# A graph-attention kernel on one core: the product with Wv of each group moved one turn later on TensorE

## The chip, the cores and the metric

The kernel runs on one core of one Trainium2 chip. The metric is the device time of one execution in microseconds (us), and the median of several runs is compared. The program is written by hand, engine by engine, with semaphores between the engines; no scheduler reorders it. The engines are named as the profile names them: PE (TensorE), ACT (ScalarE), DVE (VectorE), POOL (GpSimd, which here only issues gathers and scatters) and SP (which issues the plain DMAs).

## The reference

`x` has 100000 rows of 128 numbers, and 25000 edges run between those rows. Cut to what matters:

```
feat   = concat([h[dst], h[src], rel_pos, distance])          # per edge
z      = silu(silu(feat @ W1 + b1) @ W2 + b2)
scores = (z @ W3 + b3)[:, 0]
alpha  = softmax of the scores over the edges of one receiving row
msg    = h[src] @ Wv * (alpha * node_weight[src])[:, None]
out    = segment_sum(msg, dst)                                 # add up by receiving row
x      = layernorm(x + h + out)                                # h is x
```

So most rows are only normalised (the dense part), and the rows that receive an edge get a sum of weighted messages first.

## The kernel before

The edges are padded to 49 groups of 512 (four tiles of 128). In a first stage (turns `i`, loops over `B0`) the sender rows are gathered, multiplied with the part of W1 that belongs to them and written to DRAM, while DVE sorts the edges by receiver. In the second stage, which the change touches, the sorted edges go through a pipeline of `LAST_STEP` = 66 turns `s`. Every engine has its own loop over the same `s`, and within an engine the order of the code is the order of the work. In turn `s` PE does, for different groups, in this order:

- `krow` (L606) of group s-9: the receivers' numbers are spread over the one bank 4, from which DVE's `weights` makes the matrix `m_q`. It waits for `m_ready` of the group before, because bank 4 is the only one;
- the scores (L616) of group s-3; they wait for `x2_ready`, and in the first turn of a new batch of four groups for `s_taken`, that is until DVE's `take_scores` has read bank 3;
- the product with W2 (L623) of group s-2 and the two parts of the product with W1 (L629, L631) of group s-1;
- in one turn of four, the transpose of alpha (L639);
- z (L645) of group s-10, the sum of the weighted sender rows, into bank 5;
- the transposes of the rows of group s+1 (L596, in `turn_rows`), which ACT copies to `hkT`;
- y (L654) of group s-10, the product of z with Wv, into bank 6. It waits for ACT's copy `zs` of bank 5 (L520) of this same turn and for `y_done`, DVE's read of bank 6.

ACT does in a turn: the copy `hkT` (L500), four normalised rows of the dense part (L477), the second silu (L505, waits for the W2 product and for the scores), four more, the first silu (L510), in one turn of four an exponential (L515), the copy `zs` (L520, waits for z), five more of L477, and four rows of results (L529).

DVE does in a turn, in this order: `take_scores` (L943, one turn of four), `dense_norm` (L920), `rows` of group s-11 (L982 and L987, waits for `y_ready`), the first half of the softmax (L950 to L953, one turn of four), `dense_stats` (eight of L905, in nearly all turns up to turn 34), `weights` of group s-9 (four of L973, waits for `krow_ready`; its last one gives `m_ready`), the second half of the softmax (L959 to L964), and what is left of the running chains (short instructions of L876 to L890, some of which also lie between the others). So `rows` in turn s uses the y that PE made at the end of turn s-1.

POOL issues four gathers `r` of a later group (L415, region) once the W2 product of the third group before is done (`R_AHEAD`), then four gathers `hk` (L415, hk), and from group 39 on four scatters of results (L419) in their place. A scatter of group k waits for z of group k+25 or for the last one (`SC_AHEAD`), so the scatters that are left when the last z is done stand at the very end of the kernel. A block of the dense part comes in eight turns of nine (`DSTEP`), from the start of the second stage to turn 34.

Of the kernel before, what the change touches and what calls it, by code (L numbers as in the profile page):

```python
# [11 lines left out]
P = 128  # L12
# [3 lines left out]
TPG = 4  # L16
GE = TPG * P
G = -(-E // GE)
# [17 lines left out]
Y_LAG, Z_LAG, M_LAG = 11, 10, 9  # L36
# [81 lines left out]
def group_tiles(b):  # L118
    return min(BT, T - b * BT)


def gnn_kernel(nc, x, xw, snd_nat, rcv_nat, id_nat, signs, iota, ef_flat, w1, b1, w2, b2, w3, b3, wv, eye, out):
# [9 lines left out]
    with ExitStack() as ctx:  # L132
        def sb(name, shape, dt=F32):
            return ctx.enter_context(nc.sbuf_tensor(name, shape, dt))
# [8 lines left out]
        wvh = sb("wvh", [P, H])  # L143
# [20 lines left out]
        zs = sb("zs", [P, GE])  # L164
# [73 lines left out]
        bank = [ctx.enter_context(nc.psum_tensor(f"bank{n}", [P, GE], F32)) for n in range(8)]  # L238
# [23 lines left out]
        def wait(eng, s, n):  # L262
            if n > 0:
                eng.wait_ge(S[s], n)

        def wait_ring(eng, ring, i, per):

            if i >= 0:
                eng.wait_ge(ring[i % len(ring)], (i // len(ring) + 1) * per)
# [8 lines left out]
        def batch_of(g):  # L278
            return g // BATCH

        def batch_end(b):
            return min(b * BATCH + BATCH, G) - 1
# [260 lines left out]
        def _(pe):  # L543
# [24 lines left out]
            for i in range(B0):  # L568
                j = i - 2
                if 0 <= j < G:  # L570
# [3 lines left out]
                    for q in range(TPG):  # L574
                        to = bank[2 + j % 4][:, q * P:(q + 1) * P]
                        pe.matmul(to, hsT[:, j % 2, q * P:(q + 1) * P], w1b[:], start=True, stop=False)  # L576
                        ins = pe.matmul(to, ef[0:36, j % EF_RING, q * P:(q + 1) * P], w36[:], start=False, stop=True)  # L577
                    ins.then_inc(S["A_ready"], 1)
                if i < G:
                    wait_ring(pe, hs_in, i, 16 * TPG)  # L580
                    wait(pe, "hsT_ready", i - 1)
                    for q in range(TPG):
                        ins = pe.transpose(bank[i % 2][:, q * P:(q + 1) * P], rec[:, i % HS_RING, q, H:2 * H], ident[:])  # L583
# [8 lines left out]
            def turn_rows(g):  # L592
                wait_ring(pe, hk_in, g, 16 * TPG)
                wait(pe, "hkT_ready", g)
                for q in range(TPG):
                    ins = pe.transpose(bank[0][:, q * P:(q + 1) * P], hk[:, g, q, :], ident[:])  # L596
                ins.then_inc(S["hkT_done"], 1)

            turn_rows(0)
            for s in range(LAST_STEP):  # L600
                g = s - M_LAG
                if 0 <= g < G:
                    wait(pe, "m_ready", g)
                    for q in range(TPG):
                        t = g * TPG + q
                        ins = pe.matmul(bank[4][:, q * P:(q + 1) * P], kcol16[:, t:t + 1].to_broadcast((P, P)), ident16[:],  # L606
                                        start=True, stop=True)
                    ins.then_inc(S["krow_ready"], 1)
                g = s - 3
                if 0 <= g < G:  # L610
                    b, last = batch_of(g), g == batch_end(batch_of(g))
                    wait(pe, "x2_ready", g + 1)
                    wait(pe, "s_taken", b)
                    for q in range(TPG):
                        n = (g % BATCH) * TPG + q
                        ins = pe.matmul(bank[3][0:BT, 0:P], wz[:, BT - 1 - n:2 * BT - 1 - n], x2[:, q * P:(q + 1) * P],  # L616
                                        start=(n == 0), stop=(last and q == TPG - 1), skip_group_check=True)
                    ins.then_inc(S["score_done"], 1)
                g = s - 2
                if 0 <= g < G:  # L620
                    wait(pe, "x1_ready", g + 1)
                    wait(pe, "x2_ready", g)
                    pe.matmul(bank[2][:], w2s[:], x1[:], start=True, stop=True).then_inc(S["mm2_done"], 1)  # L623
                g = s - 1
                if 0 <= g < G:
                    wait(pe, "hkT_ready", g + 1)
                    wait_ring(pe, r_in, g, 16 * TPG)
                    wait(pe, "x1_ready", g)
                    pe.matmul(bank[1][:], w1a[:], hkT[:, g % 2, :], start=True, stop=False, skip_group_check=True)  # L629
                    for q in range(TPG):  # L630
                        ins = pe.matmul(bank[1][:, q * P:(q + 1) * P], rr[:, g % R_RING, q, 0:H], ident[:], is_transpose=True,  # L631
                                        start=False, stop=(q == TPG - 1), skip_group_check=True)
                    ins.then_inc(S["mm1_done"], 1)
                for b in range(NBATCH):
                    if batch_end(b) + 5 == s:
                        n = group_tiles(b)
                        wait(pe, "alpha_ready", b + 1)
                        wait(pe, "acol_ready", b)
                        pe.transpose(bank[7][:, 0:n], soft[0:n, 5, :], ident[0:n, 0:n]).then_inc(S["alphaT_done"], 1)  # L639
                g = s - Z_LAG  # L640
                if 0 <= g < G:
                    wait(pe, "m_ready", g + 1)
                    wait(pe, "zs_ready", g)
                    for q in range(TPG):
                        ins = pe.matmul(bank[5][:, q * P:(q + 1) * P], rr[:, g % R_RING, q, H:2 * H], m_q[:, g % 2, q, :],  # L645
                                        start=True, stop=True)
                    ins.then_inc(S["z_ready"], 1)
                if s + 1 < G:
                    turn_rows(s + 1)
                if 0 <= g < G:  # L650
                    wait(pe, "zs_ready", g + 1)
                    wait(pe, "y_done", g)
                    for q in range(TPG):
                        ins = pe.matmul(bank[6][:, q * P:(q + 1) * P], zs[:, q * P:(q + 1) * P], wvh[:], start=True, stop=True)  # L654
                    ins.then_inc(S["y_ready"], 1)

            pe.wait_ge(S["fix_in"], 16 * 11)
            for k in range(2):
                pe.transpose(bank[k][:, 0:P], yrow[:, 2 * k, :], ident[:])
                ins = pe.transpose(bank[k][:, P:T], yrow[0:T - P, 2 * k + 1, :], ident[0:T - P, 0:T - P])  # L660
# [460 lines left out]
```

## Time and profile before

| | |
|---|---|
| three runs | 1179.71, 1186.98, 1191.53 us; median 1186.98 us |
| profiled execution | 1186.11 us, of which the span that the trace covers is 1177.9 us |
| busy | PE 635.3, DVE 586.4, ACT 523.2, POOL 752.8 us |
| TensorE clock granted, mean | 0.81 |

No engine is busy for more than two thirds of the span, so waits between engines set the time. The page's 40 slices of 29.4 us each show the stages: up to slice 13 the first stage, slices 14 to 26 the second stage with dense work, from 27 on the second stage without it, and in the last five slices only POOL's scatters.

### The profile page before, as it was taken

Reading aid. Unit: us, or ns where it says so; the run is one execution under the profiler, and the core shown is the slowest. Engines: PE = TensorE matmul, PEld = TensorE weight load, DVE = VectorE, ACT = ScalarE, POOL = GpSimd, SP = SyncE. Lnnn points to the kernel's source line nnn. Section 1 sums busy time; section 2 is a strip of 40 time slices with the busy share of each in tenths; the row PEclk is TensorE's granted clock in tenths of the full one; section 3 lists DMA queues with packets and bytes.
Section 4 is the critical chain, followed back from the end, with each engine's and each line's share of the span. In section 5 each row is a group of like instructions: output and inputs, shape, how many; then the busy total and the mean of one; then the engine's idle time right before and its main releaser. Section 6 shows DMA issues by size and latency. Waiting matters only on the chain.

```text
span 1177.9 us, 11360 instructions
## 1 busy us (share of the span) xinstructions
PE 635.3 (54%) x2783; PEld 436.6 (37%) x2783; DVE 586.4 (50%) x2276; ACT 523.2 (44%) x1168; POOL 752.8 (64%) x790
## 2 busy tenths in 40 slices
PE   2388778869703445666755766665555636610000
PEld 1256555546401222444434544444344425610000
DVE  4587665564431544597657766853323135532000
ACT  0255354355522556567667858765334324340000
POOL 7566666666677565656646656664656665577775
PEclk9999999999999976787877777787778777655555
DMA  6388877879974486575747566742212211121111
GB/s 207 101 257 289 256 261 245 275 263 253 292 240 147 162 287 235 165 249 188 243 159 242 200 214 213 245 143 81 72 55 68 68 54 40 44 71 52 53 51 38
DMA packets 77913, 199.67 MB, mean 170 GB/s; under 512 B 18999, under 2 KB 49398, under 8 KB 65304
## 3 DMA queue, kind: packets, MB, share of 16 engines
q1 hardware_dynamic: 49560, 134.47, 32.0%
q0 software_dynamic: 28288, 64.48, 20.4%
q8 instruction: 23, 0.38, 0.1%
q14 instruction: 42, 0.34, 0.1%
HBM read 106.74 MB, written 92.26 MB: 169 GB/s over the span
## 4 chain that ended last, share of the span: by engine, by line
PE 22%; ACT 21%; issue 18%; another core or an unknown queue 18%; POOL 10%; DVE 7%; SPq 2%; DMA 2%; ACTq 0%; POOLq 0%; DVEq 0%
ACT xin L477 12%; POOL out_rows L419 10%; PE bank L576 8%; PE bank L583 3%; ACT hk L529 3%; PE bank L577 3%; PE bank L654 2%; DVE dst L905 2%; PE bank L616 2%; PE bank L623 1%; DMA xin<-in_x 1%; ACT x L510 1%; ACT zs L520 1%; ACT hkT L500 1%
## 5 line engine op out<-in xcount | busy, mean ns | idle before, releaser
L415 POOL DMA_INDIRECT region<-rec_d,id_t x196 | 186.5, 952 | 172.4 <-PE bank L623 53.0
L477 ACT ACTIVATE xin<-xin,drs 128x128 f32<-128x128 f32 x637 | 257.9, 484 | 52.9 <-issue 32.4
L415 POOL DMA_INDIRECT hk<-in_xw,snd_t x196 | 189.9, 969 | 102.6 <-issue 54.9
L419 POOL DMA_INDIRECT out_rows<-hk,sidx_t x196 | 188.7, 963 | 76.4 <-issue 57.8
L415 POOL DMA_INDIRECT hk<-in_x,kg_t x196 | 185.5, 946 | 66.1 <-issue 58.8
L654 PE MATMUL bank<-wvh,zs 128*128 128x128 f32 x392 | 86.5, 389 | 215.6 <-ACT zs L520 151.3
L576 PE MATMUL bank<-w1b,region 128*128 128x128 f32 x392 | 151.3, 489 | 66.3 <-issue 43.7
L905 DVE BATCH_NORM_STATS2 dst<-xin 128x6 f32<-128x256 f32 x392 | 137.6, 416 | 67.1 <-DMA xin<-in_x 50.1
L654 PEld LDWEIGHTS bank<-wvh,zs 128*128 128x128 f32 x392 | 73.4, 280 | 227.2 <-ACT zs L520 159.3
L576 PEld LDWEIGHTS bank<-w1b,region 128*128 128x128 f32 x392 | 99.1, 313 | 91.8 <-issue 56.0
L982 DVE TENSOR_TENSOR hk<-bank,hk 128x512 f32<-128x512 f32 x49 | 33.8, 689 | 185.0 <-PE bank L654 79.4
L616 PE MATMUL bank<-x,wz 128*16 128x128 f32 x392 | 79.3, 372 | 26.7 <-ACT x L505 15.9
L505 ACT ACTIVATE x<-bank,bcol 128x512 f32<-128x512 f32 x49 | 33.6, 686 | 129.4 <-remote 105.9
L487 ACT ACTIVATE region<-bank 128x512 f32<-128x512 f32 x49 | 28.9, 590 | 138.9 <-PE bank L583 61.3
L623 PE MATMUL bank<-x,w2s 128*128 128x512 f32 x98 | 72.0, 824 | 19.9 <-ACT x L510 19.3
L529 ACT ACTIVATE hk<-hk,ers 128x128 f32<-128x128 f32 x196 | 79.8, 483 | 4.6 <-issue 3.2
L973 DVE TENSOR_SCALAR m_q<-bank,kcol,acol 128x128 f32<-128x128 f32 x196 | 73.4, 403 | 2.4 <-remote 2.2
L629 PE MATMUL bank<-hkT,w1a 128*128 128x512 f32 x98 | 55.2, 647 | 20.3 <-DMA region<-rec_d,id_t 19.4
L616 PEld LDWEIGHTS bank<-x,wz 128*16 128x16 f32 x392 | 45.6, 127 | 50.2 <-issue 18.8
L583 PE MATMUL bank<-ident,hk 128*128 128x128 f32 x196 | 54.3, 432 | 16.0 <-DMA w<-hk 16.0
L645 PE MATMUL bank<-m_q,region 128*128 128x128 f32 x392 | 59.3, 297 | 1.7 <-issue 1.6
L510 ACT ACTIVATE x<-bank,bcol 128x512 f32<-128x512 f32 x49 | 33.2, 677 | 57.3 <-remote 34.7
(179 smaller groups left out, 913.0 us busy)
## 6 DMA issues: line engine op xcount, KB each, us to landing
xin<-in_x SPq DMA_DIRECT2D x49, 1024.0 KB
out_rows<-xin SPq DMA_DIRECT2D x49, 1024.0 KB
rec_d<-hk SPq DMA_DIRECT2D x49, 514.0 KB
hk<-in_xw,snd_t POOLq DMA_INDIRECT x196
hk<-in_x,kg_t POOLq DMA_INDIRECT x196
region<-rec_d,id_t POOLq DMA_INDIRECT x196
out_rows<-hk,sidx_t POOLq DMA_INDIRECT x196
ef_d<-hk SPq DMA_DIRECT2D x9, 196.0 KB
```

Of the source, the lines that this page charges most:

```text
L415: pool.indirect_dma_start(out=to, out_offset=None, in_=frm, in_offset=bass.IndirectOffsetOnAxis(ap=index, axis=0)).then_inc(done, 16)
L419: pool.indirect_dma_start(out=out, out_offset=bass.IndirectOffsetOnAxis(ap=index, axis=0), in_=frm, in_offset=None).then_inc(done, 16)
L477: ins = nc.scalar.activation(xin[:, j % X_RING, n, :], xin[:, j % X_RING, n, :], ACT.Identity, bias=drs[:, j % 2, 1, n:n + 1], scale=drs[: ...
L529: ins = nc.scalar.activation(hk[:, g, q, :], hk[:, g, q, :], ACT.Identity, scale=ers[:, b % 2, 0, n:n + 1], bias=ers[:, b % 2, 1, n:n + 1])
L576: pe.matmul(to, hsT[:, j % 2, q * P:(q + 1) * P], w1b[:], start=True, stop=False)
L583: ins = pe.transpose(bank[i % 2][:, q * P:(q + 1) * P], rec[:, i % HS_RING, q, H:2 * H], ident[:])
L616: ins = pe.matmul(bank[3][0:BT, 0:P], wz[:, BT - 1 - n:2 * BT - 1 - n], x2[:, q * P:(q + 1) * P], start=(n == 0), stop=(last and q == TPG ...
L623: pe.matmul(bank[2][:], w2s[:], x1[:], start=True, stop=True).then_inc(S["mm2_done"], 1)
L645: ins = pe.matmul(bank[5][:, q * P:(q + 1) * P], rr[:, g % R_RING, q, H:2 * H], m_q[:, g % 2, q, :], start=True, stop=True)
L654: ins = pe.matmul(bank[6][:, q * P:(q + 1) * P], zs[:, q * P:(q + 1) * P], wvh[:], start=True, stop=True)
L905: ins = vec.bn_stats(dst[:, n:n + 2, :].rearrange("p j w -> p (j w)"), xin[:, j % X_RING, n:n + 2, :].rearrange("p j h -> p h j"))
L973: ins = vec.tensor_scalar(m_q[:, g % 2, q, :], bank[4][:, q * P:(q + 1) * P], kcol[:, t:t + 1], acol[:, b % 2, n:n + 1], ALU.is_equal, ALU ...
```

## The change

Y is issued one turn later: in turn s for group s-11 in place of s-10, and at another place in the turn, after the product with W1 and ahead of the transpose of alpha and of z. Its two waits stay (the copy `zs` of its group, and DVE's read of the group before from bank 6). The banks stay as they are: one for z, one for y, one for `krow`.

```diff
@@ -631,6 +631,13 @@
                         ins = pe.matmul(bank[1][:, q * P:(q + 1) * P], rr[:, g % R_RING, q, 0:H], ident[:], is_transpose=True,
                                         start=False, stop=(q == TPG - 1), skip_group_check=True)
                     ins.then_inc(S["mm1_done"], 1)
+                g = s - Z_LAG - 1
+                if 0 <= g < G:
+                    wait(pe, "zs_ready", g + 1)
+                    wait(pe, "y_done", g)
+                    for q in range(TPG):
+                        ins = pe.matmul(bank[6][:, q * P:(q + 1) * P], zs[:, q * P:(q + 1) * P], wvh[:], start=True, stop=True)
+                    ins.then_inc(S["y_ready"], 1)
                 for b in range(NBATCH):
                     if batch_end(b) + 5 == s:
                         n = group_tiles(b)
@@ -647,12 +654,6 @@
                     ins.then_inc(S["z_ready"], 1)
                 if s + 1 < G:
                     turn_rows(s + 1)
-                if 0 <= g < G:
-                    wait(pe, "zs_ready", g + 1)
-                    wait(pe, "y_done", g)
-                    for q in range(TPG):
-                        ins = pe.matmul(bank[6][:, q * P:(q + 1) * P], zs[:, q * P:(q + 1) * P], wvh[:], start=True, stop=True)
-                    ins.then_inc(S["y_ready"], 1)
 
             pe.wait_ge(S["fix_in"], 16 * 11)
             for k in range(2):
```

The order of one turn of the second stage on PE, before, from `krow` to the next `krow` (the bracket holds the semaphores that the first instruction of a group waits for):

```order
L606 MATMUL bank<-ident,kcol 128x128 [waits m_ready]
L606 MATMUL bank<-ident,kcol 128x128 x3
L616 MATMUL bank<-x,wz 16x128 [waits s_taken,x2_ready]
L616 MATMUL bank<-x,wz 16x128 x3
L623 MATMUL bank<-x,w2s 128x512 [waits x2_ready,x1_ready]
L629 MATMUL bank<-hkT,w1a 128x512 [waits x1_ready,r_in4,hkT_ready]
L631 MATMUL bank<-ident,region 128x128 x4
L645 MATMUL bank<-m_q,region 128x128 [waits zs_ready,m_ready]
L645 MATMUL bank<-m_q,region 128x128 x3
L596 MATMUL bank<-ident,hk 128x128 [waits hkT_ready,hk_in2]
L596 MATMUL bank<-ident,hk 128x128 x3
L654 MATMUL bank<-wvh,zs 128x128 [waits y_done,zs_ready]
```

And the same stretch with the change, where y is L639 and z is L652:

```order
L606 MATMUL bank<-ident,kcol 128x128 [waits m_ready]
L606 MATMUL bank<-ident,kcol 128x128 x3
L616 MATMUL bank<-x,wz 16x128 [waits s_taken,x2_ready]
L616 MATMUL bank<-x,wz 16x128 x3
L623 MATMUL bank<-x,w2s 128x512 [waits x2_ready,x1_ready]
L629 MATMUL bank<-hkT,w1a 128x512 [waits x1_ready,r_in9,hkT_ready]
L631 MATMUL bank<-ident,region 128x128 x4
L639 MATMUL bank<-wvh,zs 128x128 [waits y_done,zs_ready]
L639 MATMUL bank<-wvh,zs 128x128 x3
L652 MATMUL bank<-m_q,region 128x128 [waits zs_ready,m_ready]
L652 MATMUL bank<-m_q,region 128x128 x3
L596 MATMUL bank<-ident,hk 128x128 [waits hkT_ready,hk_in7]
```

The four matmuls of y have gone from behind the transposes L596 to between the W1 product and z: before they stood directly ahead of `krow`, now `krow`, the scores and the products with W2 and W1 stand ahead of them in their turn.

In the turn that transposes alpha, with the change (L646 is that transpose; before, it stood directly behind L631):

```order
L629 MATMUL bank<-hkT,w1a 128x512 [waits x1_ready,r_in7,hkT_ready]
L631 MATMUL bank<-ident,region 128x128 x4
L639 MATMUL bank<-wvh,zs 128x128 [waits y_done,zs_ready]
L639 MATMUL bank<-wvh,zs 128x128 x3
L646 MATMUL bank<-ident,soft 128x16 [waits acol_ready,alpha_ready]
L652 MATMUL bank<-m_q,region 128x128 [waits zs_ready,m_ready]
```

Here y stands ahead of the one instruction in the turn that waits for the end of the softmax on DVE. On the other engines nothing moves.

## Rows read from the trace of the kernel before

**Rows 1.** Windows: stretch, length, busy of PE, PEld, DVE, ACT, POOL, clock, DMA, GB/s
```profile
491.00:784.00 293.00, 185.38 (x946) 131.57 (x946) 214.80 (x834) 207.87 (x472) 178.41 (x188) 0.77 0.62 210
784.00:983.00 199.00, 112.60 (x592) 79.14 (x591) 62.83 (x204) 75.53 (x146) 119.97 (x125) 0.75 0.24 70
```
**Rows 2.** Waits of the whole span: who waited for whom, total, times, longest
```profile
PE bank L654 <- ACT zs L520: 151.3, 34, 18.9
ACT x L505 <- remote: 105.9, 25, 9.8
```
**Rows 3.** Timeline of PE, one dense turn: start, us, engine, line, operation
```profile
671.79 2.07 PE L654 MATMUL bank<-wvh,zs 128*128 128x128 f32 x8 [3.39 <-issue]
673.65 0.63 PE L606 MATMUL bank<-ident,kcol 128*128 128x128 bf16 x4
...
675.54 1.13 PE L623 MATMUL bank<-x,w2s 128*128 128x512 f32 x2
...
677.79 1.06 PE L645 MATMUL bank<-m_q,region 128*128 128x128 f32 x8
...
684.00 2.08 PE L654 MATMUL bank<-wvh,zs 128*128 128x128 f32 x8 [4.72 <-ACT zs L520]
```
**Rows 4.** Timeline of PE, the slowest and the fastest krow-to-z seen
```profile
698.17 0.63 PE L606 MATMUL bank<-ident,kcol 128*128 128x128 bf16 x4
...
703.89 1.16 PE L645 MATMUL bank<-m_q,region 128*128 128x128 f32 x8
...
887.11 1.16 PE L654 MATMUL bank<-wvh,zs 128*128 128x128 f32 x8 [0.25 <-ACT zs L520]
888.10 0.39 PE L606 MATMUL bank<-ident,kcol 128*128 128x128 bf16 x4
...
891.65 1.06 PE L645 MATMUL bank<-m_q,region 128*128 128x128 f32 x8
```
**Rows 5.** Timeline of ACT over the same dense turn
```profile
671.16 0.58 ACT L520 ACTIVATE zs<-bank 128x512 f32<-128x512 f32 x1
...
680.68 0.69 ACT L505 ACTIVATE x<-bank,bcol 128x512 f32<-128x512 f32 x1 [3.46 <-remote]
```
**Rows 6.** Timeline of DVE: a plain turn, one without dense work, one with softmax
```profile
662.47 0.69 DVE L982 TENSOR_TENSOR hk<-bank,hk 128x512 f32<-128x512 f32 x1 [1.13 <-issue]
...
667.90 0.42 DVE L973 TENSOR_SCALAR m_q<-bank,kcol,acol 128x128 f32<-128x128 f32 x1
...
670.12 0.17 DVE L890 SCALAR_TENSOR_TENSOR drs<-dst,drs 128x16 f32<-128x16 f32 x1
...
673.90 0.69 DVE L982 TENSOR_TENSOR hk<-bank,hk 128x512 f32<-128x512 f32 x1 [2.70 <-PE bank L654]
...
675.30 1.35 DVE L973 TENSOR_SCALAR m_q<-bank,kcol,acol 128x128 f32<-128x128 f32 x4
680.62 0.34 DVE L943 TENSOR_SCALAR soft<-bank,bcol 16x128 f32<-16x128 f32 x1 [3.96 <-remote]
686.12 0.69 DVE L982 TENSOR_TENSOR hk<-bank,hk 128x512 f32<-128x512 f32 x1 [5.16 <-PE bank L654]
...
694.54 0.41 DVE L973 TENSOR_SCALAR m_q<-bank,kcol,acol 128x128 f32<-128x128 f32 x1
```
**Rows 7.** Timeline of DVE: L982 of turns 35 and 50
```profile
783.78 0.69 DVE L982 TENSOR_TENSOR hk<-bank,hk 128x512 f32<-128x512 f32 x1 [4.04 <-PE bank L654]
...
983.48 0.69 DVE L982 TENSOR_TENSOR hk<-bank,hk 128x512 f32<-128x512 f32 x1 [4.79 <-PE bank L654]
```
**Rows 8.** Timeline of POOL: the first r gathers two turns apart, a scatter
```profile
669.18 0.94 POOL L415 DMA_INDIRECT region<-rec_d,id_t  x1 [2.55 <-PE bank L645]
...
693.62 0.94 POOL L415 DMA_INDIRECT region<-rec_d,id_t  x1 [2.45 <-PE bank L645]
...
1031.93 0.96 POOL L419 DMA_INDIRECT out_rows<-hk,sidx_t  x1 [2.02 <-remote]
```
**Rows 9.** Source L982: all rows instructions, first and last start
```profile
L982 DVE TENSOR_TENSOR hk<-bank,hk x49: 668/691/693, 491.3 to 1038.0; 128x512 f32<-128x512 f32 x49
```

## The prediction

> **What bounds the kernel now.** I read the page first (no engine is busy for more than two thirds of the span), then the windows by stage, the waits, and the timeline of single turns on PE, ACT, DVE and POOL. The change touches only the second stage. From turn 11 on it has three parts. The dense part runs from the first rows instruction (L982) at 491.3 [rows 9] to that of turn 35 at 783.78 [rows 7]: 24 turns in 292.5 us, 12.2 us a turn. The part without dense work runs from there to turn 50 at 983.48: 15 turns in 199.7 us, 13.3 a turn. The last turns run to turn 59 at 1038.0 [rows 9]: 9 turns in 54.5 us, 6.1 a turn. In the first two parts PE's mean granted clock is 0.77 and 0.75 of full [rows 1], so PE changes between its two levels of 2.4 and 1.2 GHz all the time.
>
> The wait that the change removes is the longest of the table: PE's y waits for ACT's copy zs for 151.3 us in 34 waits [rows 2]. What does it hold up? In a dense turn ACT ends zs at 671.74; y starts at 671.79 [rows 3, 5], `krow` only at 673.65, behind y, and behind that come the scores and the W2 product, for which ACT's L505 then waits 3.46 us [rows 5]. Such waits of L505 are 105.9 us in 25 [rows 2]. Today's loop is thus: zs, y, krow, scores, W2 (PE), then L505, four norms, L510, zs (ACT).
>
> **What the change takes away.** With y of the group before, PE can do krow, the scores and W2 without ACT's zs of the same turn. ACT's own work of a dense turn is what is left of 12.2 us without the wait of 3.5: 8.7 us. If ACT set the pace, that would be the turn.
>
> **What it puts in its place.** DVE's loop is not moved. In its turn s, `rows` (L982) waits for y, and `weights` (L973) of the same turn comes behind it; `krow` of PE's turn s+1 waits for `m_ready` of these weights, since bank 4 is one. Before, the y that rows of turn s needs stood at the end of PE's turn s-1, ahead of krow. Now it stands in turn s, behind krow, scores, W2 and W1. So these follow each other with nothing beside them: PE krow to y (call it P), DVE rows to the last weights (D), PE krow of the next turn. Z and the transposes L596 lie beside D.
>
> D comes from the timeline of DVE [rows 6]: a plain dense turn 662.47 to 668.32, 5.8 us; a turn without dense work 673.90 to 676.65, 2.75 us; a turn with the softmax 686.12 to 694.95, 8.8 us. All of this is work or its own short chains, and L982 has no price of its own that changes (49 of about 0.69 us).
>
> P is krow, scores, W2 and W1, then y. Krow to z, which is that stretch without y, takes 3.55 us at the full clock (888.10 to 891.65) and 5.72 at its slowest (698.17 to 703.89) [rows 4]; in the turn of [rows 3] 4.14 (673.65 to 677.79). Y takes 1.0 at the full clock (887.11 to the krow behind it at 888.10) and 1.86 at half (671.79 to 673.65). So P lies between 4.6 and 7.6 us; I take 6.5, nearer to the slow end, because the mean clock is 0.77 and because ends reach others late (below). Its lower end stays the lower end of the range.
>
> Sum for the 24 dense turns. Of these, turns 17 and 26 have no dense work (every ninth), and turns 11, 15, 19, 23, 27 and 31 have the softmax:
> - 16 plain turns at 6.5 + 5.8 = 12.3: 197 us.
> - 6 with the softmax at 6.5 + 8.8 = 15.3, and 1.8 more: in these turns the scores wait for `take_scores`, which stands behind the rest of DVE's chain. The weights end at 668.32 and that chain at 670.29 [rows 6], L943 takes 0.34, so it is done 2.3 us after `m_ready`, of which krow's start covers 0.5. Together 17.1: 103 us.
> - 2 turns at 6.5 + 2.75 = 9.25, but POOL's eight gathers of a turn take 1.25 each, 10.0 us: 20 us.
>
> That is 320 us against 292.5: 27 us slower. The cover of the softmax turns was that rows never waited on the same turn's PE work; it is gone. ACT (8.7 a turn) and POOL (10.0) become the ones that wait.
>
> In the 15 turns without dense work the loop is 6.5 + 2.75 = 9.3 us (about 11 with the softmax), under the 13.3 they take. What fills those 13.3 is POOL's eight issues of 1.26 (10.1 us) and long waits on PE that I can't put down to one instruction. I cost the edit at nothing there; the bounds are -10 (a fifth of the wait was zs) and +20 (y adds its 1.0 to 1.9 on P in 13 of them, uncovered).
>
> In the last 9 turns PE only has krow, y and z. Today z, zs (0.58), y and krow follow each other, 6.1 us a turn. With the change krow, y, rows and weights do: 0.4 + 1.2 + 2.75, some 4.4 to 5.5 by the clock. But POOL issues a scatter group per turn, 4 of 1.26 = 5.0 us. I take half a microsecond a turn, 4 us less. This counts in full: at 1031.93 a scatter waits 2.02 us for PE [rows 8], and from there POOL issues without a gap to the end, so whatever moves z of the last group moves the end.
>
> The sum: +27 - 4 = +23 us. Against the profiled execution of 1186.1 us (span 1177.9 and 8.2 around it) that is 1209; that execution lies 0.9 under the median of the runs, 1186.98. Against the median it is 1210.
>
> On the clock, the trace shows 0.77 as the mean while PE is busy for 63% of the dense part [rows 1], and y takes 1.86 us in one turn and 1.0 in another [rows 3, 4]. The Trainium skill (TensorE: Matmul & The Clock Gate, Part 1) says that an array left idle falls to half its clock and that activity gives the full one back. It speaks against this change, because the loop makes PE stand still once a turn until DVE has the weights; by that rule P would sit at its slow end, and that case has its place among the rivals.
>
> **The rivals.**
> - *A, faster: ACT sets the pace after all.* P at its fast end, 4.6. Then plain turns are 4.6 + 5.8 = 10.4 (166 us for 16), softmax turns 4.6 + 8.8 + 1.8 = 15.2 (91), two of 10: 277, 15 less than now. With 8 less in the last turns it is 1164. For it: the longest wait goes. Against: the clock.
> - *B, no change: POOL keeps its beat.* The first r gathers of a turn start at 669.18 and, two turns later, at 693.62, 12.2 us a turn, though between them lie a turn with a D of 2.75 and the start of one with 8.8 [rows 6]; each time POOL waits about 2.5 us for PE [rows 8]. If that beat has a cause that I don't see, plain turns stay at 12.2 and the softmax turns' excess is made up in the others: 1187, from 1176 to 1198.
> - *C, the forecast:* the PE-DVE loop, 1199 to 1228.
> - *D, much slower: y's end comes late.* The W2 product's record ends at 676.67 and L505, which waits for it and for the scores ahead of it, starts at 680.68, 4.0 us later [rows 3, 5]. Y, with zs ahead of it, is read at once today. In the changed order y stands in the same run as W2, with W1's 1.1 to 1.3 us and its own 1.0 to 1.9 in between, so that 1.5 us of the lateness is left, in each of 24 turns: 36 more than the forecast, 1246. It decides as soon as y's end lags by more than the 0.5 us that P at 6.5 has over the sum of its rows (4.14 + 1.86).
> - *E: PE at half its clock in all of P.* P 7.6 at the slowest row: 1.1 more in 24 turns, 26: 1236.
>
> That the edit doesn't do what it says is no case: y of a group always finds its zs a turn old, and its two waits stay.
>
> **Chances.** A 0.20, B 0.24, C 0.33, D 0.16, E 0.07. A measurement of this kernel tells about 1% (12 us) from no change. Faster by over 1% is A: 0.20. Within 1% is B and a sliver of C: 0.26. Slower by over 1% is the rest: 0.54. The likeliest case gives 1210; its own range is 1199 to 1228. The range that should hold 8 in 10 leaves out half of A below and the top of D above: 1168 to 1248.
>
> **What the profile after would show.** The wait of y for zs near nothing, and in its place PE's krow waiting for DVE's L973; DVE's L982 waiting for y nearly every turn of the dense part, with 12.3 us between two of them in plain turns and 17 in turns with the softmax; L505's waits shorter or put down to krow's lateness; POOL waiting for the W2 product for longer. If rows come 10.4 apart in plain turns, A is right; if all turns stay 12.2 apart, B; if they are 13.5 or more apart with y's record ended 1.5 us before L982 starts, D. I would be wrong in the mechanism if krow doesn't wait for DVE.

## The result and the profile after

The changed kernel takes 1217.6 us (median of 4 runs, 1212.1 to 1222.0); the kernel before took 1187.8 beside it (4 runs, 1179.7 to 1191.5). The ratio is 1.029, with a 95% interval from 1.024 to 1.034: 30 us slower, where the likeliest case said 23. The profiled execution is the slowest of the four, 1222.0 us with a span of 1214.5, so the two traces differ by 36.6 us, more than the medians. TensorE's mean clock is 0.79 (0.81 before).

Where the 36.6 us are is read from DVE's `rows`, the same instruction as in [rows 7, 9] (from here on the lines of DVE are one higher, y is L639 and z L652). Its first and last start:

```profile
L983 DVE TENSOR_TENSOR hk<-bank,hk x49: 669/692/693, 488.0 to 1074.1; 128x512 f32<-128x512 f32 x49
```

Turn 35 now starts at 824.8 and turn 50 at 1019.8. The window of the dense part, with the columns of [rows 1]; the clock in it is 0.74, where it was 0.77:

```profile
488.00:825.00 337.00, 203.80 (x967) 129.30 (x967) 214.40 (x834) 218.95 (x488) 184.19 (x195) 0.74 0.56 188
```

The dense part took 336.8 us for 24 turns, 44.3 more than before (forecast 27). The part without dense work took 194.9, 4.8 less (forecast 0); the last turns 54.3, 0.3 less (forecast 4). The start of the stage came 3.3 earlier and the end of the kernel 0.5 later; together that is 36.6. So the whole loss lies in the dense turns. Of the 44 us, 8 come from y's end being seen late in two of them (told with rival D below).

The waits answer to [rows 2]; "remote" is a releaser that the trace doesn't name. Columns: who waited for whom, total us, times, longest:

```profile
PE bank L606 <- DVE m_q L974: 116.8, 26, 14.3
DVE hk L983 <- PE bank L639: 116.7, 29, 7.3
DVE hk L983 <- remote: 116.2, 11, 15.8
...
PE bank L606 <- issue: 100.9, 19, 12.0
...
ACT x L505 <- remote: 36.6, 9, 6.4
...
ACT x L505 <- PE bank L623: 29.5, 19, 3.2
```

The 151 us of y waiting for `zs` are gone from the head of the table (15.0 are left), and L505 waits less: it had 105.9 us under this releaser, now 36.6, and 29.5 of short ones (0.9 us in a plain turn) for the W2 product. In their place PE's `krow` waits for DVE's weights (the row with "issue" too: in the turns below it starts 0.06 us behind them), and DVE's rows wait for y. One plain turn and the start of a softmax turn on PE, against [rows 3]:

```profile
745.87 0.61 PE L606 MATMUL bank<-ident,kcol 128*128 128x128 bf16 x4 [4.66 <-issue]
746.40 1.89 PE L616 MATMUL bank<-x,wz 128*16 128x128 f32 x8
748.22 2.08 PE L623 MATMUL bank<-x,w2s 128*128 128x512 f32 x2
750.09 1.91 PE L629 MATMUL bank<-hkT,w1a 128*128 128x512 f32 x2
751.80 0.70 PE L631 MATMUL bank<-ident,region 128*128 128x128 f32 x4
752.33 1.06 PE L639 MATMUL bank<-wvh,zs 128*128 128x128 f32 x8
...
759.16 0.61 PE L606 MATMUL bank<-ident,kcol 128*128 128x128 bf16 x4 [4.44 <-issue]
761.48 1.86 PE L616 MATMUL bank<-x,wz 128*16 128x128 f32 x8 [1.72 <-issue]
```

And DVE over the same time, against [rows 6]:

```profile
745.40 0.41 DVE L974 TENSOR_SCALAR m_q<-bank,kcol,acol 128x128 f32<-128x128 f32 x1
753.42 0.69 DVE L983 TENSOR_TENSOR hk<-bank,hk 128x512 f32<-128x512 f32 x1 [4.76 <-PE bank L639]
758.70 0.40 DVE L974 TENSOR_SCALAR m_q<-bank,kcol,acol 128x128 f32<-128x128 f32 x1
761.00 0.33 DVE L944 TENSOR_SCALAR soft<-bank,bcol 16x128 f32<-16x128 f32 x1
767.79 0.69 DVE L983 TENSOR_TENSOR hk<-bank,hk 128x512 f32<-128x512 f32 x1 [5.68 <-PE bank L639]
```

Read the two side by side. The last weights end at 745.81, `krow` starts at 745.87. Y's record ends at 753.39, rows start at 753.42. The weights end at 759.10, `krow` starts at 759.16. Each waits for the other, with nothing of the loop beside it (z and the transposes L596 lie beside D, as foreseen): P (krow to the end of y) is 7.5 us, D (rows to the last weights) 5.7. The scores start at 761.48, behind `take_scores` (L944), 1.7 us late.

### The profile page after: what moved, and what is told of

Read it like the earlier page. It is cut to its first block, busy times and chain, and to the rows that moved or that the text cites. A ratio compares the mean times of both kernels' runs of the same rounds, so it can differ in the third digit from the quotient of the medians.

```text
span 1214.5 us, 11360 instructions
## 1 busy us (share of the span) xinstructions
PE 640.9 (53%) x2783; PEld 422.9 (35%) x2783; DVE 586.0 (48%) x2276; ACT 526.9 (43%) x1168; POOL 752.6 (62%) x790
## 4 chain that ended last, share of the span: by engine, by line
PE 22%; DVE 20%; issue 16%; another core or an unknown queue 12%; POOL 8%; ACT 4%; DMA 1%; DVEq 0%; POOLq 0%; SPq 0%; ACTq 0%
POOL out_rows L419 8%; PE bank L623 5%; PE bank L616 4%; DVE dst L906 4%; PE bank L629 3%; DVE m_q L974 3%; PE bank L639 3%; ACT xin L477 2%; DVE hk L983 2%; PE bank L606 2%; PE bank L631 1%; DVE est L988 1%; PE bank L652 1%; PE bank L576 1%
## 5 line engine op out<-in xcount | busy, mean ns | idle before, releaser
L983 DVE TENSOR_TENSOR hk<-bank,hk 128x512 f32<-128x512 f32 x49 | 33.9, 691 | 257.9 <-PE bank L639 116.7
L606 PE MATMUL bank<-ident,kcol 128*128 128x128 bf16 x196 | 26.4, 279 | 219.9 <-DVE m_q L974 116.8
L606 PEld LDWEIGHTS bank<-ident,kcol 128*128 128x128 bf16 x196 | 15.3, 120 | 230.8 <-DVE m_q L974 122.9
L623 PE MATMUL bank<-x,w2s 128*128 128x512 f32 x98 | 88.4, 999 | 12.8 <-issue 12.5
L629 PE MATMUL bank<-hkT,w1a 128*128 128x512 f32 x98 | 72.0, 827 | 32.4 <-DMA region<-rec_d,id_t 26.8
L974 DVE TENSOR_SCALAR m_q<-bank,kcol,acol 128x128 f32<-128x128 f32 x196 | 73.3, 402 | 0.3
L520 ACT ACTIVATE zs<-bank 128x512 f32<-128x512 f32 x49 | 28.9, 590 | 99.7 <-remote 72.4
L639 PE MATMUL bank<-wvh,zs 128*128 128x128 f32 x392 | 58.3, 296 | 15.7 <-ACT zs L520 15.0
L652 PE MATMUL bank<-m_q,region 128*128 128x128 f32 x392 | 59.7, 296 | 6.5 <-issue 6.5
L505 ACT ACTIVATE x<-bank,bcol 128x512 f32<-128x512 f32 x49 | 33.6, 685 | 67.4 <-remote 36.6
```

Source lines behind the costliest of these rows:

```text
L974: ins = vec.tensor_scalar(m_q[:, g % 2, q, :], bank[4][:, q * P:(q + 1) * P], kcol[:, t:t + 1], acol[:, b % 2, n:n + 1], ALU.is_equal, ALU ...
```

## The experiments

The kernels were timed in four series, each beside the kernel before. That one took 1180 us in the series of `stats_behind`, `before_stats_behind`, `lag12` and `y_scores`, 1184 in that of `weights_first`, `lag12_wfirst`, `y_end` and `warm`, 997 in that of `early_take`, `wfirst_take_alpha` and `lag12_wfirst_take_alpha`, and 1181 beside `wfirst_take_alpha_2`; the 997 are taken up below. The changed kernel itself was timed only beside the 1188, with a ratio of 1.029. So a difference from it is given by the ratios, as a share of 1188 us; the medians alone can differ from that by some 8 us. "Dense part" is the time from the first rows instruction to that of turn 35.

**Dense statistics behind the weights, on the changed kernel.**
```diff
-                dense_stats(u)
                 if 0 <= s - M_LAG < G:
                     weights(s - M_LAG)
+                dense_stats(u)
```


> The changed kernel, with DVE's eight dense_stats instructions put behind weights in its turn; nothing is left out. Theory (PE-DVE loop: krow to y on PE, then rows to weights on DVE): D falls from 5.8 to about 2.8 us in plain turns, so a plain turn falls from 13.4 us to about 10.5, where POOL's eight gathers (10.1) take over; the turns with the softmax keep about 16, since take_scores now comes behind more work. The 24 dense turns fall from 337 us to about 285, the time to about 1165 (1155 to 1185). Rival (the clock of PE or ACT's later copies set the 13.4 us): the order inside DVE doesn't matter, 1210 to 1225.

Measured: 1190.8 us, ratio 1.012 (1.005 to 1.020). The dense part fell from 336.8 to 308.5 us. Of the forecast 52 us, 27 came by the medians and 20 by the ratios: the plain turns did shrink, the softmax turns did not. DVE, with rows (L983) and weights (L974):

```profile
510.90 0.69 DVE L983 TENSOR_TENSOR hk<-bank,hk 128x512 f32<-128x512 f32 x1 [10.65 <-remote]
...
520.19 0.69 DVE L983 TENSOR_TENSOR hk<-bank,hk 128x512 f32<-128x512 f32 x1 [0.27 <-PE bank L639]
521.79 1.37 DVE L974 TENSOR_SCALAR m_q<-bank,kcol,acol 128x128 f32<-128x128 f32 x4
530.44 0.69 DVE L983 TENSOR_TENSOR hk<-bank,hk 128x512 f32<-128x512 f32 x1 [0.83 <-remote]
531.84 1.35 DVE L974 TENSOR_SCALAR m_q<-bank,kcol,acol 128x128 f32<-128x128 f32 x4
538.49 0.33 DVE L944 TENSOR_SCALAR soft<-bank,bcol 16x128 f32<-16x128 f32 x1
546.17 0.69 DVE L983 TENSOR_TENSOR hk<-bank,hk 128x512 f32<-128x512 f32 x1 [6.59 <-PE bank L639]
```

D is now 3.0 us, and two plain turns are 10.3 apart. In the first of them DVE's own work fills 9.4 us (520.19 to 529.61), so DVE is near its own bound there. The first turn of the part is 23.2 us long: y's record ended at 498.87, and DVE stood for 10.65 us before it started rows at 510.90. Such late ends add up to 16.3 us in the dense part, against 9.2 in the changed kernel. And the statistics now stand between the weights and `take_scores` of the next turn, which starts 5.3 us behind the end of the weights (1.9 in the changed kernel); the scores wait for it, and the next turn is 15.7.

**The same edit on the kernel before**, as a control.

> The kernel before, with the same move of dense_stats behind weights; nothing is left out. A control. Theory: before the change DVE's rows-to-weights path was not in the loop that sets the turn (zs, y, krow, scores, W2, L505), so the time stays at 1175 to 1195. If DVE's order were worth as much here as in the changed kernel (50 us), the loop would not be what the change brought in.

Measured: 1176.8 us, ratio 0.998 (0.994 to 1.003). No change, as the theory has it: before the change, D isn't in the loop that sets the turn.

**Rows one turn later as well**, which opens the loop at y (y stands behind the transpose of alpha here, so that no engine waits in a circle).
```diff
-Y_LAG, Z_LAG, M_LAG = 11, 10, 9
+Y_LAG, Z_LAG, M_LAG = 12, 10, 9
```


> The changed kernel with rows (and all that follows it: its chain, results, stores) one turn later (Y_LAG 12), so that rows in turn s uses the y of turn s-1; y also stands behind the transpose of alpha, without which the last batches would wait for each other. PE still doesn't wait for zs of its own turn. Theory: the PE-DVE loop is open, and krow waits only for weights that wait for no y of the same turn. A plain turn goes to 10 to 11 us (POOL's 10.1, ACT's 8.7), the time to 1150 to 1180. Rival 1 (POOL keeps a beat of 12.2 whatever PE does): 1180 to 1192, as before the change. Rival 2 (y's place in the run of PE is what costs): 1210 to 1225.

Measured: 1166.0 us, ratio 0.990 (0.983 to 0.997): by the ratios 47 us less than the changed kernel, and a little under the kernel before. Rows no longer wait for the same turn's PE work: most plain turns are 8.5 to 9.5 us.

**The weights ahead of rows**, which opens the loop at `krow` (with them the multiplication that makes `acol`).
```diff
+                if 0 <= s - M_LAG < G:
+                    weights(s - M_LAG)
                 if 0 <= s - Y_LAG < G:
                     rows(s - Y_LAG)
...
-                if 0 <= s - M_LAG < G:
-                    weights(s - M_LAG)
```


> The changed kernel with DVE's weights (and the copy of alpha's column that they need) ahead of rows in its turn. PE is as in the change: y behind W1. Theory: krow of the next turn waits for weights, and these no longer wait for y, so the loop is open; a plain turn goes to POOL's bound or to the 12.2 us that the kernel before keeps, the time to 1160 to 1190. Rival (y's place on PE is what costs): 1210 to 1225.

Measured: 1168.1 us, ratio 0.987 (0.980 to 0.993). DVE of this kernel:

```profile
618.00 0.68 DVE L983 TENSOR_TENSOR hk<-bank,hk 128x512 f32<-128x512 f32 x1
625.89 1.36 DVE L974 TENSOR_SCALAR m_q<-bank,kcol,acol 128x128 f32<-128x128 f32 x4
627.21 0.69 DVE L983 TENSOR_TENSOR hk<-bank,hk 128x512 f32<-128x512 f32 x1
```

A plain turn is 9.2 us, against 13.1 to 13.6 in the changed kernel, with the same work on every engine. In that turn ACT is busy for 9.19 of 9.20 us, so ACT sets it. By the ratios the gain on the changed kernel is 50 us. What stays long are the turns at the softmax (most of them 13.1 to 16, the first 22.2).

**Both openings together.**

> Both openings together: rows one turn later and weights ahead of rows. Theory: once the loop is open, opening it twice gives little; the next bound is POOL's gathers and its wait for PE, as in lag12: 1155 to 1175, within 1% of lag12. Rival (DVE's order still holds krow up in the turns with the softmax): 15 to 25 us less than lag12, 1140 to 1150.

Measured: 1165.1 us, ratio 0.985 (0.979 to 0.991), within the intervals of either alone. One loop was there; opened at either end it is gone, and a second opening finds nothing.

**Y directly behind the scores**, so that W2 and W1 leave P.
```diff
                     ins.then_inc(S["score_done"], 1)
+                g = s - Z_LAG - 1
+                if 0 <= g < G:
+                    wait(pe, "zs_ready", g + 1)
+                    wait(pe, "y_done", g)
+                    ...
                 g = s - 2
```


> The changed kernel with y directly behind the scores, ahead of the W2 and W1 products. Theory: P, the stretch from krow to y on PE, falls by W2 and W1, 3.5 to 4 us of 7.5; a plain turn goes from 13.4 to about 10.2 (POOL's bound), the time to 1155 to 1180. Rival (it is the wait of rows for anything in the same turn, through ACT's zs, that costs): y now comes earlier and meets zs sooner, so PE waits for zs again as before the change, 1187 or more.

Measured: 1193.8 us, ratio 1.013 (1.005 to 1.020), slower than the expected 1155 to 1180. With P shorter by W2 and W1, plain turns should have come near 10; most came at 12.2. PE, DVE and POOL show why (here y is L624, W2 L630):

```profile
728.68 2.08 PE L624 MATMUL bank<-wvh,zs 128*128 128x128 f32 x8
730.55 1.20 PE L630 MATMUL bank<-x,w2s 128*128 128x512 f32 x2
```
```profile
733.16 0.69 DVE L983 TENSOR_TENSOR hk<-bank,hk 128x512 f32<-128x512 f32 x1 [3.43 <-remote]
```
```profile
721.70 0.95 POOL L415 DMA_INDIRECT region<-rec_d,id_t  x1 [2.57 <-PE bank L630]
...
730.47 0.94 POOL L415 DMA_INDIRECT hk<-in_x,kg_t  x1 [0.30 <-issue]
733.93 0.94 POOL L415 DMA_INDIRECT region<-rec_d,id_t  x1 [2.52 <-PE bank L630]
```

Y's record ends at 730.76, rows start at 733.16, 2.4 us later. W2 ends at 731.75, POOL sees it at 733.9. POOL's eight gathers (721.70 to 731.41) and a pause of 2.5 make 12.2: the beat of rival B, in a kernel whose PE-DVE loop is shorter. The PE-DVE loop with its late end comes to about as much there (P 3.9, 2.4 until rows start, D 5.6: 12.0), so which of the two holds the turn isn't separated.

**Y at the end of the turn** (up to turn 49), behind z and the transposes, so that P grows by both.

> The changed kernel with y (still of group s-11) at the end of PE's turn, behind z and the transposes, up to turn 49; from turn 50 on it stands where the change put it. Theory (PE-DVE loop): the stretch from krow to y grows by z and the transposes, about 2 us in each of 24 dense turns; plain turns 15.4 instead of 13.4 us, the time 1245 to 1265. Rival (the change costs because y stands ahead of z and so delays zs and the results): putting it behind z gives the time back, 1185 to 1215.

Measured: 1264.3 us, ratio 1.070 (1.063 to 1.078). The dense part took 367 us. The size came as expected, not its split. P did not grow by 2 us: it was 7.8 to 8.1 in plain turns, most of which were 13.6 to 13.9 apart. So z and the transposes added 1.3 us ahead of y, but the first part of W1 (L629) took 1.02 at the full clock, where it took 1.91 in the changed kernel. The two turns at the softmax were 16 and 18, and one turn was 20, in which y was seen 9.6 us late.

**PE kept busy through its standstill:** ten matmuls of constants (64 by 384, bf16) into an unused part of bank 3 behind the transposes in each turn. They add work that the result doesn't use (where `warm16` is set up isn't shown).
```diff
                 if s + 1 < G:
                     turn_rows(s + 1)
+                if 7 <= s < G + 9:
+                    for _ in range(10):
+                        pe.matmul(bank[3][64:P, P:4 * P], ident16[:, 0:64], warm16[:], ...)
```


> The changed kernel with ten additional bf16 matmuls (64x384, into a quarter of bank 3 that nothing reads) behind the transposes of every turn, in the time in which PE stands waiting for DVE's weights. Nothing is left out. In the trace of the change krow, scores, W2 and W1 run at the half clock (krow to y 7.5 us). If the clock falls because PE stands still there, the added work keeps it up: P falls towards 4.9 us, plain turns from 13.4 to 11 or 12.2, the time to 1160 to 1195, at a higher mean clock. If the clock is not set by that standstill, nothing changes or the added work costs: 1215 to 1235.

Measured: 1209.9 us, ratio 1.025 (1.016 to 1.033), against 1.029 (1.024 to 1.034) without them: a gain in time isn't shown, and the expected 1160 to 1195 was missed. The turns can be read all the same. The mean clock from 488 to 780 us rose from 0.74 to 0.82. PE, two turns of this kernel (y is L640, the added ones L660):

```profile
732.00 0.40 PE L607 MATMUL bank<-ident,kcol 128*128 128x128 bf16 x4 [2.30 <-DVE m_q L979]
732.33 1.05 PE L617 MATMUL bank<-x,wz 128*16 128x128 f32 x8
...
735.57 1.06 PE L640 MATMUL bank<-wvh,zs 128*128 128x128 f32 x8
...
737.88 1.81 PE L660 MATMUL bank<-warm,ident 128*64 128x384 bf16 x10
742.58 0.40 PE L607 MATMUL bank<-ident,kcol 128*128 128x128 bf16 x4 [2.88 <-issue]
...
743.88 1.98 PE L624 MATMUL bank<-x,w2s 128*128 128x512 f32 x2
```

In the first turn P is 4.6 us (732.00 to 736.63) and the turn 10.6 from krow to krow, so the loop does shrink by what the clock gives back. In the second the clock fell at W2 all the same. The dense part of the two traces differs by 11 us (325.7; the fastest execution of this kernel, the slowest of the changed one). Only some turns were warm, the softmax turns kept their waits, and in turn 18 DVE started rows 11.8 us behind the end of y's record.

**`take_scores` one turn earlier**, behind rows, for batches 0 to 11.

> The changed kernel with one edit on DVE: take_scores of batches 0 to 11 stands one turn earlier, directly behind rows (which waited for y, and y stands behind these scores on PE, so it waits for nothing new). My theory (the loop PE krow to y, DVE rows to weights, plus about 1.8 us in a softmax turn, in which the scores wait for take_scores behind DVE's chain): PE's 1.7 us of idle ahead of L616 in these turns goes, take_scores' 0.34 us comes onto the turn before; the turn with the softmax and the one behind it get about 1.5 us shorter together, and more if the scores' lateness had also held up the exponential. 12 batches, so 15 to 30 us off 1217.6: 1188 to 1203, likeliest 1198. Rival (the loop goes through ACT or POOL, and the wait on take_scores lies beside another one): within 5 us of 1217.

Measured: 1060.9 us, ratio 1.064 (1.062 to 1.066), in the series where the kernel before takes 997. Its 1060.9 can't be set against 1217.6; the ratio is far above the 1.029 of the changed kernel, which neither theory had foreseen. The turns can be compared, for the plain ones are still 12.8 to 13.7 apart. PE and DVE:

```profile
651.67 0.61 PE L606 MATMUL bank<-ident,kcol 128*128 128x128 bf16 x4 [4.66 <-DVE m_q L974]
...
654.03 2.08 PE L623 MATMUL bank<-x,w2s 128*128 128x512 f32 x2
...
658.29 1.06 PE L639 MATMUL bank<-wvh,zs 128*128 128x128 f32 x8
```
```profile
645.72 0.69 DVE L983 TENSOR_TENSOR hk<-bank,hk 128x512 f32<-128x512 f32 x1 [4.92 <-PE bank L639]
...
659.39 0.69 DVE L983 TENSOR_TENSOR hk<-bank,hk 128x512 f32<-128x512 f32 x1 [4.88 <-PE bank L639]
```

P is 7.7 us (651.67 to 659.35) and D 5.9, as in the changed kernel. Of the softmax turns, the distances to the turn before and behind are 13.7 and 15.0 (659.4, 673.0, 688.1), where the changed kernel has 14.4 and 16.5: 2.2 us less a pair. That is not the wait of 1.7 as such: P of turn 31 is 7.7, against 8.6 with the wait in it, so the wait cost 0.9 (behind it the first part of W1 took 1.27 in place of 1.91), and 1.1 more comes from P of turn 32, 6.3 against 7.4. The other pairs are 0.9 to 3.0 us shorter.

**The weights first, `take_scores` early, and the transpose of alpha one turn later** on PE (directly behind `krow`, for all batches but two; in the second kernel rows stand one turn later as well, and `take_scores` behind `dense_stats`):
```diff
                 for b in range(NBATCH):
-                    if batch_end(b) + 5 == s:
+                    if b < NBATCH - 2 and batch_end(b) + 6 == s:
```


> weights_first (1168 us) with two edits: take_scores one turn earlier behind rows, as in early_take, and the transpose of alpha one turn later on PE, directly behind krow, for all but the last two batches. In weights_first plain turns were 9.0 to 9.4 apart and the two turns at the softmax 13.4 to 16; in its trace PE stands 5.4 us ahead of the transpose of alpha until DVE has ended the softmax, and the scores wait for take_scores in the turn before. If these two waits are all that lengthens those turns, they fall to 10 to 13 us (DVE has about 13 us of work in a softmax turn), 12 batches times 4 to 7 us: 1085 to 1130. If POOL's eight gathers (10.0 us) with their wait of 2.2 to 2.5 us set a beat of 12.2 us, as they do in the kernel before and in y_scores, most is eaten: 1150 to 1170. Likeliest 1130.

> The same two edits on lag12_wfirst (1165 us; rows one turn later as well; take_scores behind dense_stats). If the loop from y to rows is already open in wfirst_take_alpha, this gives the same within 1%; if a beat of 12.2 us comes in as in lag12, it is slower than wfirst_take_alpha by 10 to 30 us. Likeliest 1135, 1090 to 1165.

Measured in the series of the 997: 996.6 us, ratio 1.000 (0.999 to 1.001), and 997.1 for the one with rows later too. Both were expected some 4 to 5% under the kernel before (1130 and 1135 us beside 1184) and both missed. With the kernel before, all three take the same, and the page of the first says what that time is:

```profile
L415 POOL DMA_INDIRECT hk<-in_xw,snd_t x196 | 188.0, 959 | 62.0 <-issue 59.1
L419 POOL DMA_INDIRECT out_rows<-hk,sidx_t x196 | 188.4, 961 | 59.8 <-issue 57.3
L415 POOL DMA_INDIRECT region<-rec_d,id_t x196 | 186.2, 950 | 59.7 <-issue 57.3
L415 POOL DMA_INDIRECT hk<-in_x,kg_t x196 | 185.6, 947 | 59.7 <-issue 58.8
```

Busy and idle of the four lines add up to 989.4 of a span of 994.1 us, and all but some 9 us of the idle time are the 0.3 us between two issues. POOL hardly waits: 784 issues at 1.25 us, 980 us, are the floor of this program. That the kernel before stands on the same floor there is concluded from its 996.8 us; there is no trace of it in that series.

**The same kernel once more.**

> The same kernel as wfirst_take_alpha, once more, because the kernel before took 996.8 us on the chip of that run and 1180 to 1187 on the others; in those other traces PE's ends reach their waiters up to several us after their records, in that one never. If the kernel before takes about 1180 here: the two waits that this version removes are worth something only as far as the late ends leave room; weights_first was 1168, so 1120 to 1165 if they are, likeliest 1145; 1165 to 1180 if the late ends set a beat of 12.2 us again. If the kernel before takes about 997 here: 995 to 999 again, since POOL then issues its 788 gathers and scatters at 1.25 us each, 985 us, nearly without a gap.

Measured: 1173.4 us beside 1181.0, ratio 0.995 (0.991 to 0.998). The kernel before was at 1181 again, and this version, at POOL's floor in the series of the 997, is no better than `weights_first` here (0.987). The time lies in the expected 1165 to 1180, but not by a beat of 12.2 us: plain turns are 9.1, and most batches have one turn of 20 to 23. ACT and POOL in one of them:

```profile
592.90 0.31 ACT L515 ACTIVATE soft<-soft 16x128 f32<-16x128 f32 x1 [0.38 <-issue]
602.95 0.60 ACT L520 ACTIVATE zs<-bank 128x512 f32<-128x512 f32 x1 [9.74 <-remote]
```
```profile
599.10 0.95 POOL L415 DMA_INDIRECT hk<-in_x,kg_t  x1 [0.30 <-issue]
```

Z, for which `zs` waits, has its record end at 588.29 in that trace. ACT is free from 593.21 and starts `zs` at 602.95, 14.7 us behind that end, and 2.9 us after POOL's run of gathers has ended with the one shown.

## Why the prediction was right, and where it was not

**The mechanism (case C) was right.** PE's krow to y and DVE's rows to weights follow each other with nothing beside them; the trace shows the two hand-overs at 0.03 to 0.06 us. Two edits that share nothing but that loop, at either end of it, take 47 and 50 us away by the ratios, and both together 52, no more than the intervals allow for either. The same edit of D takes 20 to 27 us from the changed kernel and nothing that can be told from the one before (0.998, 0.994 to 1.003).

**D was right:** 5.6 to 5.9 in plain turns (5.8), 8.5 to 9.1 with the softmax (8.8; one 9.7, and 6.8 in turn 11), 2.8 to 3.0 without dense work (2.75).

**P was sized too small: the term that failed.** I took 6.5 us; in most plain turns it is 7.3 to 7.7 (7.5 in the one above). Krow, the scores, W2 and W1 run at the low clock, y at the full one: scores 1.89 and W2 2.08 in the plain turn above, against 1.05 and 1.13 in the warm turn of the kernel with added matmuls. Ahead of them PE stood still for 4 to 4.7 us in the plain turns. Behind the two turns without dense work it stood for under 2 us, and P was 4.6 there, all of it at the full clock. That is the mechanism that I had set apart as rival E with 7.6 us and a chance of 0.07, and it is no rival but a part of C: the loop makes PE stand, and standing makes P long. Added up over the 24 turns, P with the late scores in it is 177.5 us, 10.7 more than the sum had; D is 148.6, 2.5 less, of which turn 11 is 2.0; late ends of y are 8.3 in two turns; the hand-overs of 0.04 and 0.06 us make 2.5; and 2 us of the 320 were POOL's bound in the turns without dense work and rounding. That is how the dense part came out 17 us longer. The Trainium skill (TensorE: Matmul & The Clock Gate, Part 1) has the rule that an idle array falls to half its clock. The trace agrees, at 1.9 and 2.1 us against 1.05 and 1.13. By that rule the plain turns would have been sized rightly; the total would not, since 7.6 us in all 24 turns gave 1236, farther from 1217.6 than 1210 is.

**That the total came within 8 us of 1210 is in part luck.** The dense part was 17 us longer than forecast, half of it by late ends for which the sum had no term, and the last turns gained 4 us less. Against that stand 5 us less in the part without dense work, 3 us less ahead of the first rows, and medians that lie 7 us nearer to each other than the two traces.

**The softmax turns** came as a sum: 14.4 and 16.5 us for the pair, 30.9, against 17.1 and 12.3. The late scores of 1.8 us were 1.7 of standing, of which 0.9 counted in P, as `early_take` shows.

**The turns without dense work** were forecast at no change and gained 4.8 us, inside the bounds of -10 and +20. **The last turns** were forecast at 4 less and gained 0.3: they are 6.0 us apart, not 5.5.

**Rival A** (ACT sets the pace, 10.4 us a plain turn) is excluded: plain turns are 13.1 to 13.6.

**Rival B** (POOL's beat of 12.2) is not what the changed kernel does, but the beat exists. It is seen in `y_scores`, and in the series of the 997 it isn't there.

**Rival D** (y's end late by 1.5 us) is excluded for the plain turns: DVE starts 0.03 us behind the record of y. Without late ends, in `early_take`, nearly all of these turns are as long, 12.8 to 13.7 us. But its mechanism did act in two of the 24 turns, 18 and 27, each behind a turn without dense work, by 6.6 and 1.8 us. Turn 18, PE and DVE:

```profile
577.15 1.06 PE L639 MATMUL bank<-wvh,zs 128*128 128x128 f32 x8
...
584.80 0.69 DVE L983 TENSOR_TENSOR hk<-bank,hk 128x512 f32<-128x512 f32 x1 [11.27 <-remote]
```

Y's record ends at 578.21. So that turn, forecast at 10.0, came at 14.2.

**What the edit was good for** was true in the waits: y hardly waits for `zs`, ACT waits less for the W2 product. With the loop opened the plain turn is 9.2 us, and the whole 1 to 1.5% under the kernel before. How much of that is owed to the move of y is not shown: no run has the weights ahead of rows, or rows one turn later, without it. And the dense part is no shorter than before (296.3 us in `weights_first`, 295.4 in `lag12`, against 292.5), because the turns at the softmax grew by what the plain ones lost; the gain lies in the part without dense work (180.3 and 173.2 against 199.7). So the change needs at least its second half on DVE.

## What to carry to other kernels

If an operation is moved behind others on its engine, write down the circle that its result closes: who waits for it, what that engine has to do before it frees the next thing this engine waits for, and whether both stretches now lie end to end. If they do, the turn is their sum, and one of the two has to be turned round (here the weights ahead of rows) in the same edit. Size the stretch on TensorE at its low clock when the circle makes TensorE stand still once a turn as it did here.

## What the runs showed of the hardware

**The same kernel, 997 or 1180 us, by the series.** Within a series the times hold together (21 runs from 995.8 to 997.8 us in that of the 997). Whether the chip is the cause is not shown: the four series ran on chips numbered 7, 9, 7 and 2, so the first series, with 1180 us, and the third, with 997, carry the same number. The instructions are as long in both (POOL's gathers 0.95 to 0.97 us each). What differs in the traces is when a finished instruction is seen by the others. In the trace of the kernel before, the W2 product ends at 676.67 and ACT starts 4.0 us later [rows 3, 5]. In the series of the 997 the same pair, W2 of `early_take` above, ending at 656.11:

```profile
656.14 0.69 ACT L505 ACTIVATE x<-bank,bcol 128x512 f32<-128x512 f32 x1 [0.84 <-PE bank L623]
```

Set against the semaphore events of the traces, each PE instruction's end in the second stage and the next event of its semaphore: in `early_take` all of 343 ends have their event within 0.02 us. In the kernel before it depends on where the end falls in a run of POOL's gathers without a pause: of 57 ends in the first 4 us of a run 5 are seen more than 0.5 us late, of 39 ends 8 to 10 us into one all are, by 2.7 us in the median, and 37 of them 1.5 to 3.5 us after the run has stopped. In the changed kernel, whose POOL pauses for 2.4 to 8.3 us in nearly each dense turn, it is 2 of 96 and 15 of 26. These counts are rough: only 292 of the 343 ends of the kernel before have an event of their own in the trace (284 in the changed one), and events more than 9 us behind were left out as doubtful. That the waiting engines really stand is read from their rows.

It reaches the first stage too, which the change doesn't touch. There POOL's gathers of sender rows, kernel before and then `early_take` (busy, mean ns, idle time before and its causes):

```profile
L415 POOL DMA_INDIRECT hk<-in_xw,snd_t x196 | 189.9, 969 | 102.6 <-issue 54.9 <-PE bank L583 23.2 <-remote 21.9
```
```profile
L415 POOL DMA_INDIRECT hk<-in_xw,snd_t x196 | 188.8, 963 | 62.0 <-issue 58.8 <-DMA snd_t<-in_snd_nat 2.6 <-PE bank L583 0.6
```

45 us of waits for PE and for a releaser that the trace doesn't name are 0.6 there, and the first rows instruction comes at 410.8 instead of 491.3. The beat of 12.2 us is then what two things add up to: ten us of gathers, and the 2.5 us until POOL sees the W2 product that ended inside them. That POOL's issuing is what holds the ends back was not tried by changing its order. In the other series they go together. In `early_take` they don't, though 93 of its ends fall more than 8 us into a run of gathers; so the gathers alone are not the cause, and what else differs between the series stays open. The Trainium skill (Perfetto Trace Analysis, Tensor Engine Instruction) says that the recorded end of a matmul is an estimate and that its semaphore follows; it has no figure for the gap. Here it is 0.01 us in the series of the 997, and in the others an engine with nothing else to do started up to 11.8 us behind the recorded end (rows behind y, turn 18 of the kernel with added matmuls).

**The cost of this change may depend on that.** Beside `lag12` the kernel before is 183 us above its time beside `early_take`. A longer turn, in which POOL pauses, has fewer late ends, so part of the longer loop may have been paid back; how much is not measured. In the series of the 997 even the version with early `take_scores` is 6.4% slower; the changed kernel itself was not run there.
